# Macaron block on one core: norm rows transposed by DMA, a third buffer for the probabilities, and operation orders by the slot's place in the batch

## The reference

```python
x = x + 0.5 * ffn(layernorm(x), W_up, W_gate, W_down)
x = x + attention(layernorm(x), wq, wk, wv, wo)
x = x + 0.5 * ffn(layernorm(x), W_up, W_gate, W_down)
```

## Time and profile before

| | |
|---|---|
| median of the runs | 716.58 us |
| profiled execution | 718.6 us |
| its span, first to last instruction | 716.7 us |
| mean granted TensorE clock | 0.951 of full speed |
| TensorE, ScalarE, VectorE, GpSimd busy | 608.3, 592.4, 573.9, 542.8 us |
| packets of the SP queue | 87.06 MB |

### The profile page before, as it was taken

One profiled execution on the slowest core, in us unless ns is written; L12 is line 12 of the kernel. 1 busy time (PEld: TensorE's weight loads), 2 busy tenths in 40 slices (PEclk: granted clock), 3 DMA queues, 4 the chain that ended last, 5 costly groups with the idle time before them and its releaser, 6 DMA issues. The chain is left out here.

```text
span 716.7 us, 16950 instructions
## 1 busy us (share of the span) xinstructions
PE 608.3 (85%) x5961; PEld 476.3 (66%) x5961; DVE 573.9 (80%) x1448; ACT 592.4 (83%) x1179; POOL 542.8 (76%) x581
## 2 busy tenths in 40 slices
PE   1679858789999999999999999999999787878586
PEld 1367626567777787868787877777778565556365
DVE  2977566878989999998989898989898777776653
ACT  4256578889999999999999999999999878888742
POOL 3246576879898998989898989797989867675632
PEclk9999978999999999999999999999999788897889
DMA  8501467775757675758585857676775778786700
GB/s 329 185 25 30 60 113 131 126 140 117 159 115 140 116 163 101 164 99 178 104 168 96 166 111 148 131 130 132 133 148 119 163 111 148 129 141 119 129 1 30
DMA packets 311573, 90.43 MB, mean 126 GB/s; under 512 B 301761, under 2 KB 310209, under 8 KB 311489
## 3 DMA queue, kind: packets, MB, share of 16 engines
q1 hardware_dynamic: 310624, 87.06, 61.8%
q10 hardware_dynamic: 864, 2.29, 0.9%
HBM read 9.63 MB, written 4.19 MB: 19 GB/s over the span
## 5 line engine op out<-in xcount | busy, mean ns | idle before, releaser
L686 ACT ACTIVATE prob<-score_ps,exp_bias,exp_scale 128x128 f32<-128x128 f32 (+1 forms) x512 | 224.4, 513 | 15.8 <-DVE exp_bias L944 14.7
L1087 POOL TENSOR_TENSOR prob_hl<-prob,prob_hl 128x768 f16<-128x768 f32 x128 | 211.0, 1648 | 20.3 <-ACT prob_hl L697 20.3
L1092 POOL TENSOR_TENSOR hid_l<-hid,hid_h 128x512 f16<-128x512 f32 x128 | 149.3, 1166 | 91.9 <-ACT hid_h L706 91.1
L414 PE MATMUL down_ps<-tern_down,hid_h 128*128 128x256 f16 x512 | 120.1, 275 | 18.1 <-POOL hid_l L1092 16.1
L414 PE MATMUL down_ps<-tern_down,hid_l 128*128 128x256 f16 x512 | 119.9, 274 | 0.0
L697 ACT ACTIVATE prob_hl<-prob 128x768 f16<-128x768 f32 x128 | 107.9, 843 | 9.0 <-DMA raw_w<-prob_hl 8.4
L706 ACT ACTIVATE hid_h<-hid 128x512 f16<-128x512 f32 x128 | 81.2, 635 | 38.9 <-DVE hid L980 38.8
L971 DVE SCALAR_TENSOR_TENSOR silu_b<-tanh_b,up_ps 128x512 f32<-128x512 f32 x128 | 87.1, 681 | 24.8 <-ACT tanh_b L701 24.6
L701 ACT ACTIVATE tanh_b<-up_ps,tanh_scale 128x512 f32<-128x512 f32 x128 | 87.7, 685 | 21.5 <-PE up_ps L414 21.2
L980 DVE SCALAR_TENSOR_TENSOR hid<-silu_b,gate_ps 128x512 f32<-128x512 f32 x128 | 88.0, 687 | 17.0
L422 PE MATMUL score_ps<-mask_b,ident_b 128*128 128x256 bf16 x256 | 73.3, 287 | 26.9 <-ACT prob L686 26.6
(11 more groups left out here) (106 smaller groups left out, 1359.2 us busy)
## 6 DMA issues: line engine op xcount, KB each, us to landing
xs<-x SPq DMA_DIRECT2D x16, 256.0 KB, 2.8
out<-xs SPq DMA_DIRECT2D x16, 256.0 KB, 2.8
raw_w<-prob_hl SPq DMA_TRANSPOSE x128, 3.7
raw_up<-w_up_t ACTq DMA_DIRECT2D x1, 512.0 KB, 5.1
raw_up<-w_up_t SPq DMA_DIRECT2D x1, 512.0 KB, 6.8
raw_gate<-w_gate_t ACTq DMA_DIRECT2D x1, 512.0 KB, 7.3
raw_gate<-w_gate_t SPq DMA_DIRECT2D x1, 512.0 KB, 8.9
raw_down<-w_down_t ACTq DMA_DIRECT2D x1, 512.0 KB, 9.9
```

The source lines that it names most:

```text
L414: mm = pe.matmul(dst, lhs, rhs, start=flags and n == 0, stop=n == len(pairs) - 1, skip_group_check=True)
L686: e = act.activation(prob[:, n % 2, at + j * width:at + (j + 1) * width], score_ps[:, n % 2 if tile else 2, j * width:(j + 1) * width], AC ...
L1087: pool.tensor_tensor(prob_hl[:, n % 2, 1, :], prob[:, n % 2, :], prob_hl[:, n % 2, 0, :], ALU.subtract).then_inc(prob_l_done, 1)
L1092: pool.tensor_tensor(hid_l[:, n % 2, :, :].rearrange("p m n -> p (m n)"), hid[:, n % 2, :], hid_h[:, n % 2, :, :].rearrange("p m n -> p (m ...
```

## The change

- **Norms.** ScalarE applies a norm straight into `misc_ps`, copies it from there to float16 rows `x_row` (high part), VectorE makes the low part of the rows, and SP issues one transposing DMA of 128 x 1024 (`turn_norm`). TensorE's transposes of the norms are gone. Row buffers are single, transposed ones double for all three norms (norm 2 had one).
- **Third buffers** for `prob`, `prob_hl` and `prob_t`, in memory of raw weights that is free by then; the waits of `exps`, `prob_hi` and `turn_probs` go three pairs back.
- **Moves.** The high parts of the turned `attn` and of v go from ScalarE to VectorE.
- **Plan.** `AHEAD` 3 instead of 4, `FIRST_FFN` -18 instead of -16, other slots for the norms and their steps, for v and for the set-up of the weights. `scores_1` is issued one slot ahead of its pair.
- **Orders.** Each of the four engines has one order below slot 0 and eight for the others, by `g % 8` (a ninth, behind `else`, is never reached). On SP the order is `turn_rows`, `turn_norm` of the next slot, `turn_probs` of this slot's pair, store, load.
- **Loads.** x from batch 2 on is loaded nine slots ahead of its first ffn. The first halves of `raw_down` and `raw_w`, and the rotary tables, are issued by ScalarE instead of SP.
- On GpSimd only orders change, besides the semaphores that follow from the above. Waits of several VectorE operations stand in another order.

```diff
-FIRST_FFN = -16
-AHEAD = 4
+FIRST_FFN = -18
+AHEAD = 3
...
-PT_BUFS = 2
-SUM_UP_AT = FIRST_FFN - 4
-SUM_GATE_AT = FIRST_FFN - 3
-SUM_DOWN_AT = FIRST_FFN + 0
-SPLIT_HI_AT = FIRST_FFN + 4
+LOAD_AHEAD = 9
+PT_BUFS = 3
+SUM_UP_AT = FIRST_FFN - 5
+SUM_GATE_AT = FIRST_FFN - 1
+SUM_DOWN_AT = FIRST_FFN - 1
+SPLIT_HI_AT = FIRST_FFN + 3
...
-SPLIT_LO_AT = FIRST_FFN + 4
-CASTS_AT = FIRST_FFN + 8
+SPLIT_LO_AT = FIRST_FFN + 8
+CASTS_AT = FIRST_FFN + 17
...
-OF_BATCH = [("norm2", -8, "a"), ("qk0", -8, "b"), ("qk1", -6, "a"), ("v", -3, "b"),
-            ("attn_t", 10, "b"), ("out_proj", 11, "b"), ("norm3", 13, "b")]
+OF_BATCH = [("norm2", -10, "b"), ("qk0", -8, "a"), ("qk1", -6, "a"), ("v", -4, "b"),
+            ("attn_t", 10, "b"), ("out_proj", 11, "b"), ("norm3", 12, "b")]
...
-              [(FFN_START[1, b] - 1, "a", "norm1", b) for b in range(NBATCH)])
+              [(FFN_START[1, b] - 2, "a", "norm1", b) for b in range(NBATCH)])
...
-    1: {"stats": 4, "mean": 4, "var": 8, "power": 4, "shift": 4, "apply": 3},
-    2: {"stats": 3, "mean": 3, "var": 0, "power": 3, "shift": 3, "apply": 1},
-    3: {"stats": 1, "mean": 1, "var": 20, "power": 2, "shift": 2, "apply": 1},
+    1: {"stats": 3, "mean": 3, "power": 3, "shift": 3, "turn": 0},
+    2: {"stats": 2, "mean": 2, "power": 2, "shift": 1, "turn": 0},
+    3: {"stats": 1, "mean": 0, "power": 0, "shift": 0, "turn": 0},
...
# SP
+            def turn_norm(k, b):
+                last = b - XT_BUFS[k]
+                sp.wait_ge(misc_taken, through(f"norm{k}", b))
+                if last >= 0 and k == 2:
+                    sp.wait_ge(misc_written, max(through("qk1", last), through("v", last)))
+                elif last >= 0:
+                    sp.wait_ge(up_done, ROUNDS * added(1 + k // 2, last))
+                    sp.wait_ge(gate_done, ROUNDS * added(1 + k // 2, last))
+                sp.dma_start_transpose(xt[k][:, b % XT_BUFS[k], :, :, :, :].rearrange("p n a c q -> p (n a c) q"),
+                                       x_row[k][:, :, :, :].rearrange("p n a e -> p (n a e)")).then_inc(xt_turned[k], 16)
...
             def slot(g):
-                for n in pair_of(g, 1):
-                    turn_probs(n)
                 for b, tile in events(g, ROW_LO):
                     turn_rows(b, tile)
+                for k, b in norms(g - -1, "turn"):
+                    turn_norm(k, b)
+                for n in pair_of(g, 0):
+                    turn_probs(n)
...
# TensorE
-                pe.wait_ge(misc_taken, through(f"norm{2 * f - 1}", b))
+                pe.wait_ge(xt_turned[2 * f - 1], 16 * (b + 1))
...
+                elif g % SLOTS == 2:
+                    for n in pair_of(g, 0):
+                        scores_0(n)
+                    for name, b in uses_of(g, "a"):
+                        misc(name, b)
+                    for r in round_of(g, 0):
+                        up(*r)
+                    for n in pair_of(g, 3):
+                        product_v(n)
+                    for n in pair_of(g, -1):
+                        scores_1(n)
+                    for r in round_of(g, 0):
+                        gate(*r)
...
# ScalarE
             def misc(name, b):
                 if name.startswith("norm"):
                     k = int(name[-1])
-                    split_misc(name, b, xt_hi[k][:, b % XT_BUFS[k], :, :], X_SCALE, xt_hi_done[k])
-                elif name == "attn_t":
-                    split_misc(name, b, attn_h[:, :, :], 1.0, attn_h_done)
...
+                    act.wait_ge(shift_done[k], b + 1)
+                    act.wait_ge(misc_taken, through(name, b) - 1)
+                    for tile in range(NT):
+                        a = act.activation(misc_ps[:, tile * E:(tile + 1) * E], x_rows(b, tile * E, E), ACT.Identity,
+                                           bias=shift[k][:, tile:tile + 1], scale=rstd[k][:, tile:tile + 1])
+                    a.then_inc(misc_written, 1)
+                    if b:
+                        act.wait_ge(xt_turned[k], 16 * b)
                     act.wait_ge(misc_written, through(name, b))
...
+                    act.activation(x_row[k][:, :, 0, :], misc_ps[:, :].rearrange("p (n e) -> p n e", n=NT), ACT.Copy,
+                                   scale=X_SCALE).then_inc(xt_hi_done[k], 1)
...
-                    act.wait_ge(prob_turned[(n - 2) % PT_BUFS], 16 * ((n - 2) // PT_BUFS + 1))
...
+                if n >= PT_BUFS:
+                    act.wait_ge(prob_turned[n % PT_BUFS], 16 * (n // PT_BUFS))
...
# VectorE
+                    dve.wait_ge(xt_hi_done[k], b + 1)
+                    dve.scalar_tensor_tensor(out=x_row[k][:, :, 1, :], in0=misc_ps[:, :].rearrange("p (n e) -> p n e", n=NT),
+                                             scalar=X_SCALE, in1=x_row[k][:, :, 0, :], op0=ALU.mult, op1=ALU.subtract
+                                             ).then_inc(misc_taken, 1)
                 elif name == "attn_t":
-                    low_part(b, attn_l[:, :, :], attn_h[:, :, :], 1.0, attn_h_done)
+                    dve.wait_ge(misc_written, through(name, b))
+                    dve.tensor_copy(attn_h[:, :, :].rearrange("p c n -> p (c n)"), misc_ps[:, :]).then_inc(attn_h_done, 1)
+                    dve.wait_ge(attn_h_done, b + 1)
+                    dve.tensor_tensor(attn_l[:, :, :].rearrange("p c n -> p (c n)"), misc_ps[:, :],
+                                      attn_h[:, :, :].rearrange("p c n -> p (c n)"), ALU.subtract).then_inc(misc_taken, 1)
...
                 elif name == "v":
                     v = v_row[:, b % 2, :, :]
+                    dve.wait_ge(misc_written, through(name, b))
+                    dve.tensor_scalar(v[:, :, 0:HD], misc_ps[:, :].rearrange("p (m d) -> p m d", d=HD), QKV_OUT, None,
+                                      ALU.mult).then_inc(v_hi_done, 1)
                     dve.wait_ge(v_hi_done, b + 1)
```

762 lines of the change are left out of this document (661 added, 101 removed).

## The result

| | before | after |
|---|---|---|
| median, measured side by side | 716.49 us (715.99 to 716.74) | 707.56 us (707.18 to 710.32) |
| profiled execution | 718.6 us | 707.76 us |
| its span | 716.7 us | 705.8 us |

The ratio is 0.9885 (95% interval 0.9859 to 0.9910): faster by 1.2%, 9 us, where 20.5 were forecast. Of the 10.9 us between the two spans some 2 are the profiled execution of before, which lay 2 us above its median. Measured again later, the unchanged kernel after stood at 0.9841 (0.9806 to 0.9876) against before, 1.6%. So the gain is 9 to 11 us, and ratios taken at different times that are 0.004 apart tell nothing.

The account below looks back on a forecast made before the run. It took work on four nearly full engines to bound the full stretch, the pair-to-pair loop the thin stretches, and a chain each end. Terms -6 - 3 - 8 - 1 - 3.5 + 1 = -20.5 us gave 696.0 us, range 678 to 712.

Parts of the forecast that it names:

- Full stretch: Ten full batches, 165 to 542 us: a batch falls from 37.7 to 36.9 us, 8 us gained.
- VectorE at 96%: Sign in the full stretch: VectorE becomes the busiest engine at 96%, with ScalarE and TensorE at 93%.
- TensorE's relief: Full batches: the norms' float transposes leave TensorE, 1.3 us less a batch, 35.7 to 34.4.
- The rival built on it: Full stretch: no gain there, the busy engine merely changes; 708 us in all, chance 0.14.
- Prologue: Up to the first probabilities: four rounds leave, scores at 79.5 us, probabilities at 86; 6 us gained.
- the first probabilities' low part, 6.7 us later: End of the prologue: distance from first scores to the first probabilities' low part, 85.5 to 92.3 us in the earlier trace.
- Last 15 slots: Thin stretch before the tail: third buffer and earlier score product take it from 60.6 to 57 us, 3.5 gained.
- the first two batches: Thin stretch behind the prologue: third buffer and earlier score product take it from 72.7 to 69.7 us, 3 gained.
- Batches 12 and 13: Thin stretch behind the full batches: takes two new rounds each, absorbed by gaps; 73.1 to 72 us, 1 gained.
- Tail: Behind the last probabilities: norm 3's transposes become a 3.3 us transfer, partly offset by earlier steps; 1 us lost.
- The queue: Transposing DMA queue: 48 norm transfers of 3.3 us cost nothing; share 0.68 to about 0.78 in the full stretch.
- Rival (c): SP queue: norm transfers delay the probabilities' transfers and value products wait; slower, 34 us more, 730 us, chance 0.10.

Follow-up runs that it names:

- the run that gives the load back: Kernel after plus four float32 transposes of a constant block, taken by nobody, in three slots of each batch behind the value product: 714.80 us, 0.9964.
- the reordered run: Kernel after with GpSimd's hidden_lo ahead of rope_add below slot 0: 706.09 us, 0.9833; measured again 708.62 us, 0.9859.
- the run with the filled gap: Kernel after plus 60 float32 transposes of a constant block, taken by nobody, behind the first v product: 711.80 us, 0.9916.
- one exchange: Kernel after with the probabilities' transfer issued ahead of the next slot's norm transfer on SP's queue: 723.29 us, 1.0082.
- one doubling: Kernel after with each of the 48 norm transfers followed by a second of the same size that nobody reads: 739.92 us, 1.0304.

## Why the prediction was right and wrong

**Full stretch: right in its time (-8 against -7.7; a batch of 36.6 to 37.2 us but for one of 37.9), in part wrong in its reasons.** "TensorE 34.4, ScalarE 34.7, VectorE 35.6" came out as 34.6, 35.2 and 34.9. The two moves took less from ScalarE's busy time (0.74 us a batch, not 1.2) and gave less to VectorE's (0.69, not 1.4) than the instructions' durations, and in the kernel before with the moves alone it is the same (0.64 and 0.77). The working added durations to busy times, and these are not the same sum. The records of neighbouring instructions overlap:

```profile
81.07 0.69 DVE L1178 SCALAR_TENSOR_TENSOR x_row<-misc_ps,x_row 128x512 f16<-128x512 f32 x1 [4.63 <-ACT x_row L812]
81.68 0.28 DVE L1052 CAST mask_b<-mask_f 128x256 bf16<-128x256 f32 x1
```

Over the ten full batches of before VectorE's durations add up to 392.7 us in 342.0 us of busy time, and with the moves alone to 405.8: 1.3 us more a batch in durations, as forecast, in 0.77 us of busy time. So ScalarE remained the busiest and VectorE at 96% did not come. TensorE's relief, first in my working, is worth 1.9 us of the 7.7 by the run that gives the load back, the third buffer 2.4 by its own run. The remaining 3.4 (2.0 if before's profile was 1.4 us slow) belong to the orders, the earlier norms and the moves together, and these can't be told apart by undoing one: in the orders of after each absence costs more than the whole gain. That share stays open. The -7.7 against -8 is thus in part luck. The waits of the earlier trace rows fell as forecast, the value products' wait of 7.3 us came in, and the busy times that set the 36.9 us are not those that came.

I had rejected a rule of the Trainium skill with the sentence "the columns are the load". 11.0 us more of TensorE's matmuls cost 1.9 us. The page Perfetto Trace Analysis (Identifying the Most-Contended Engine) of the Trainium skill has TensorE's headroom judged by its weight loads and its share of peak arithmetic, not by matmul busy time, and for this stretch the runs are nearer to it than to me. The rival built on it was written as "-20.5 + 8 = 708", a slip: 716.6 - 20.5 + 8 is 704. Neither number counts for it, since its mechanism did not come: the full stretch did gain its 8 us, and the missing ones are elsewhere.

**Prologue: the step that failed first (-6 forecast, -1.3 measured, -3.0 in the second profile).** "That round starts about 2.5 us sooner than 68.7, and is through TensorE at 68. From there: ... together 11.8 us." The length was right: from the product at 70.58 to the scores at 82.61 are 12.0 us. The start was not: round 11 was through TensorE at 68.4, nearly as forecast, but the product stood 2.6 us later than 68 (0.9 in the second profile), in line behind a down product that waited 1.3 us for its low part, which GpSimd made late; that product and its wait are in no term of the sum. (The terms add up to 79.8 us, where the text has 79.5.) Nor would it have helped to be on time, as the reordered run shows: the way to the scores grew by 1.5 us. The sum counts GpSimd's work for one tile, 3.8 us, and GpSimd has the other tile's low parts (2.4 us) and the rounds' in the same row; that this row is what holds the chain is argued from the timelines, not shown by a run. The second failed part is "the first probabilities' low part, 6.7 us later": it was 8.4, of which the run with the filled gap attributes 1.2 to the clock. The gap that I opened by taking out the rounds lowered it: TensorE had nothing to do for 7.6 us, and its granted clock was 0.59 from 80 to 98 us, where it was 0.91 in the same window of before. The kernel before with `AHEAD = 3` agrees, though its gap is shorter (2.4 us):

```profile
79.37 0.59 PE L424 MATMUL score_ps<-k_pad,q_stk 128*128 128x512 f16 x1
```

Its first scores stand at 79.3 us, near the 79.5 of the forecast, and the first probabilities' low part comes 8.8 us behind them. With the rounds back in the kernel after, a pause of 4.4 us ahead of the last down product leaves the first scores at half the clock as well (0.42 and 0.63 us), and the low part 7.3 us behind them. The page TensorE: Matmul & The Clock Gate of the Trainium skill (Part 1: The HAM clock gate) ties the lower clock to idle gaps; the trace agrees, and I had not asked it of a gap that the change itself opens. What AHEAD gives by itself is 4.2 us, not 6, and other edits of the prologue gave 1.2 to 2.9 back.

**Last 15 slots: the second failed step (-3.5, +0.3).** "The third buffer and the earlier score product work on these." They don't: without the one the end is as long, without the other too. TensorE's waits for transposed probabilities in this stretch, the two rows of after (601.9 to 662.8 us) and that of before (615.1 to 675.7):

```profile
PE pv_ps L482 <- DMA raw_gate<-raw_gate: 4.4, 2, 3.0
...
PE pv_ps L482 <- DMA raw_w<-prob_hl: 4.1, 3, 3.3
```

```profile
PE pv_ps L464 <- DMA raw_w<-prob_hl: 6.0, 5, 3.0
```

They are 8.5 us, where they were 6.0, and take back what the scores' wait for the exponentials gained (from 5.5 us to 3.7). These waits are for data, by the time from exponential to landing, and a buffer doesn't shorten that. Timeline of after, TensorE, from there into the tail:

```profile
661.88 0.52 PE L482 MATMUL pv_ps<-v_row,raw_gate 128*128 128x33 f16 x12 [2.97 <-DMA raw_gate<-raw_gate]
...
664.65 0.52 PE L482 MATMUL pv_ps<-v_row,raw_w 128*128 128x33 f16 x12 [2.25 <-DMA raw_w<-prob_hl]
...
668.13 1.89 PE L432 MATMUL up_ps<-raw_up,tern_up 128*128 128x256 f16 x8 [2.96 <-DMA raw_up<-x_row]
```

In the first two batches the stretch gained 1.3 and 0.2 us in the two profiles, where 3 were forecast. The buffer's own part there can't be told from the differences between profiles, and what is missing stays open.

**Batches 12 and 13: right in sign, too small (-1, -2.9).** I charged the four rounds and let gaps absorb them. They cost nothing, and the clock is at 0.99 where it was 0.84. That they shorten the stretch is not shown: in the kernel before the same four rounds make it 73.7 us instead of 73.1, at a clock of 0.95 instead of 0.84.

**Tail (+1, +2.0).** The chain from the last sum of out_proj to the first up product is 11.0 us (676.37 to 687.34), 1.3 more than the 9.7 of the earlier trace rows; the forecast had 2.7 less 1. The other 0.8 us lie ahead of that sum (662.8 to 676.4, against 675.7 to 688.4). The value products did wait 0.7 less there, as forecast. But a second norm 3, that of batch 14, has its transfer there too, and no term of the forecast has it: the up product comes 3.5 us behind the value product ahead of it (668.13), 2.9 before (681.07). The last probabilities' transfer stands behind it in the queue, issued at 666.69 with its low part ready at 664.4, and the last value product waits for it. The clock is no difference there, since that up product took 1.89 us before as well. The one long wait ahead of an apply is in the tail too (3.0 us, for GpSimd's shift, with a tanh behind it). In the full stretch, where I allowed 0.1 us a norm for the taker of the bank, ScalarE doesn't wait ahead of an apply at all: the 7.0 us in its group's row are the prologue's and the tail's.

**The queue.** "In the full stretch to about 0.78": it was 0.89, although the queue's share over all (73% against 71) was near. The share can't be worked out from the bytes: the same transfers of before, at 134 and 135 GB/s, show 0.68 in one kernel's profile and 0.78 in another's (`AHEAD = 3`), and after shows 0.89 at 164. The transfer itself was over-priced, 2.7 us from issue to landing and not 3.3. "The cost is nothing as long as this gap is there" holds for the transfers as they stand. That the gap is "almost two slots (9 us)" does not: it is 4.1 to 6.4 us, and exchanging two issues used it up. Rival (c) was thus near, one exchange or one doubling away.

**Subtraction.** I put the sum on the median, and 2 of the 10.9 us of the spans were the profiled execution of before being slow, so the median gained 9. And a measurement does not tell 0.2%, as I wrote: the same kernel stood at 0.9885 and at 0.9841.
